# A four-layer transformer with all five engines' orders written in a table: the table is laid out anew

## What is computed

```
x = x + L0_xattn(ctx, ctx, layernorm(x))   # one head, softmax over 120 context rows
x = x + L0_ffn(layernorm(x))               # 8 heads x 8 experts for v and for o, top-2 gates, 128x128 attention
x = x + L1_xattn(layernorm(x), ctx)        # 16 heads, padding masks
x = x + L1_ffn(layernorm(x))               # ternary weights, gelu, 512 hidden
x = x + L2_xattn(layernorm(x), ctx)        # 2 heads, normalised q and k, pair mask
x = x + L2_ffn(layernorm(x))               # 8 experts, top-2, gelu
x = x + L3_xattn(layernorm(x), ctx, bias)  # 16 heads of 64
x = x + L3_ffn(layernorm(x))               # grouped top-2 of 8 experts, relu squared, plus a shared part
```

## Time and profile before

| | us |
|---|---|
| median of 3 executions | 735.09 (734.54 to 735.96) |
| the profiled execution's own time | 735.45 |
| its span, first to last instruction | 734.1 |
| busy: TensorE, VectorE, ScalarE, GpSimd | 666.4, 526.9, 381.2, 197.5 |

### The profile page before, as it was taken

How to read it: one execution, slowest core, us unless ns; L and a number is a source line. 1 busy time by engine, 2 the same in 40 slices (tenths; PEclk the granted TensorE clock), 3 DMA queues, 4 the chain that set the end, 5 groups by cost and what they waited for, 6 DMA issues and landing times.

```text
span 734.1 us, 14783 instructions
## 1 busy us (share of the span) xinstructions
PE 666.4 (91%) x5494; PEld 590.2 (80%) x5494; DVE 526.9 (72%) x1449; ACT 381.2 (52%) x1295; POOL 197.5 (27%) x260
## 2 busy tenths in 40 slices
PE   5859997989999899888999999888999999788987
PEld 4649995759999788667999998577999999467876
DVE  3956657878677928987885677888884777646756
ACT  3431205772354842885457640876538531667583
POOL 1000226411215512532333311622413110542140
PEclk9889999899999989999999999999999999799989
DMA  9859993029963603007755464005766272000000
GB/s 333 332 160 362 397 379 99 2 75 357 319 221 116 230 1 90 3 4 263 272 187 165 147 230 149 1 12 202 243 212 209 101 232 78 5 1 0 2 1 12
DMA packets 34199, 113.86 MB, mean 155 GB/s; under 512 B 4560, under 2 KB 8272, under 8 KB 33744
## 3 DMA queue, kind: packets, MB, share of 16 engines
q1 hardware_dynamic: 34128, 112.92, 43.8%
HBM read 111.86 MB, written 1.05 MB: 154 GB/s over the span
## 4 chain that ended last, share of the span: by engine, by line
PE 65%; DVE 15%; ACT 10%; DMA 4%; POOL 3%; issue 2%; SPq 0%; DVEq 0%; ACTq 0%
PE f_bank L441 31%; PE bank L441 28%; DMA gated<-gates_of 3%; PE bank L679 3%; ACT wide_b L1110 3%; ACT f_b L1018 2%; DVE wide_b L1416 2%; POOL wide_b L1317 2%; DVE max_neg L1675 2%; DVE gated L1413 2%; ACT wide_a L961 1%; DVE f_route L1413 1%; DMA wide_b<-in_raw0f 1%; DVE x L1416 1%; ACT f_a L961 1%
## 5 line engine op out<-in xcount | busy, mean ns | idle before, releaser
L441 PE MATMUL f_bank<-weights,gated 128*128 128x128 f32 x2048 | 246.4, 278 | 7.6 <-DVE gated L1413 7.6
L441 PEld LDWEIGHTS f_bank<-weights,gated 128*128 128x128 f32 x2048 | 236.7, 193 | 11.1 <-issue 8.3
L1110 ACT ACTIVATE wide_b<-wide_b,max_neg 128x120 f32<-128x120 f32 x272 | 103.5, 385 | 22.2 <-DVE max_neg L1768 14.0
L1317 POOL TENSOR_TENSOR wide_b<-wide_b,row_inv 128x480 f32<-128x480 f32 x64 | 69.5, 1091 | 116.2 <-DVE row_inv L1680 116.1
L1413 DVE TENSOR_TENSOR gated<-gated,f_b 128x1024 f32<-128x1024 f32 x64 | 81.2, 1291 | 18.0 <-DMA gated<-gates_of 8.9
L1413 DVE TENSOR_TENSOR gated<-gated,f_xnT 128x1024 f32<-128x1024 f32 x64 | 77.1, 1225 | 19.2 <-DMA gated<-gates_of 18.4
L1309 POOL TENSOR_TENSOR rstd<-var_eps,w_const 128x1 f32<-128x1 f32 (+1 forms) x48 | 35.8, 749 | 194.3 <-DVE var_eps L1409 194.2
L961 ACT ACTIVATE wide_a<-bank 120x512 f32<-120x512 f32 (+4 forms) x110 | 59.3, 544 | 51.9 <-PE bank L679 24.5
L679 PE MATMUL bank<-w_const,wide_b 128*120 128x128 f32 x256 | 44.4, 307 | 14.3 <-POOL wide_b L1317 14.2
L679 PEld LDWEIGHTS bank<-w_const,wide_b 128*120 128x120 f32 x256 | 32.0, 153 | 26.5 <-issue 16.9
L1110 ACT ACTIVATION_READ_ACCUMULATOR wide_b<-wide_b,max_neg 128x1 f32 x272 | 51.8, 190 | 0.0
(11 more groups left out here) (248 smaller groups left out, 1261.7 us busy)
## 6 DMA issues: line engine op xcount, KB each, us to landing
gated<-gates_of SPq DMA_DIRECT2D x128, 512.0 KB, 5.6
weights<-in_experts SPq DMA_DIRECT2D x64, 512.0 KB, 6.3
w_L2f<-in_L2f SPq DMA_DIRECT2D x1, 2124.0 KB, 14.6
w_L3x<-in_L3x SPq DMA_DIRECT2D x1, 2108.0 KB, 18.5
wide_b<-in_raw0f SPq DMA_DIRECT2D x1, 1024.0 KB, 7.3
w_L3f<-in_L3f SPq DMA_DIRECT2D x1, 1000.0 KB, 21.2
w_L1f<-in_L1f SPq DMA_DIRECT2D x1, 516.0 KB, 10.3
x_next<-in_x SPq DMA_DIRECT2D x4, 128.0 KB, 4.9
```

Of the source, the lines that this page charges most:

```text
L441: return nc.tensor.matmul(o, lhsT, rhs, start=first, stop=last)
L1110: last = nc.scalar.activation(p, p, ACT.Exp, bias=max_neg[lane][:, h:h + 1], accum_out=row_sum[lane][:, h:h + 1])
L1317: nc.gpsimd.tensor_tensor(p3, p3, row_inv[lane][:, 4 * i:4 * i + 4].unsqueeze(2).broadcast_to([128, 4, K]), ALU.mult).then_inc(probs_norme ...
```

## The change

Nothing but the table `ORDER` changes. All five strings are written anew; each keeps its length, and each stream keeps its steps and their order within the stream, so every engine executes the same steps as before. What changes is how the three streams are interleaved. The first line of TensorE's string, for example:

```diff
-    "PE": "fff0ffffff0f0f0ffff0ffff0f00fff0ffffffffffff0fffffffffffffffffffffffffffff0f010f1fff0f0ff10f00f1fff0"
+    "PE": "ffffffffff00f0fffffffff0f0ff00fffff00ffffff0fffffffffffffffffffffffffffffff0010f1ff0fff1f0f010f0f0f0"
```

More of the change, by code:

```diff
@@ L63 @@
-    "Pool": "fff0010fff0ff01101001f0f111000111110000110101010110101101010ffff0f0100f0f101111000111100100010000101"
-          "10010111111ff0fff0110000ff101101011010100010010100001110111111ff100f1111100f001111000101010000100011"
+    "PE": "ffffffffff00f0fffffffff0f0ff00fffff00ffffff0fffffffffffffffffffffffffffffff0010f1ff0fff1f0f010f0f0f0"
+          "fff0ff011ff101fff11f1ff1ff01101001010f0ff0ff0f01f01f1ff01f100f1ff1f001f1f0110f1f100010f1f0f11010101f"
+          "110f1fff0f1f110f1f1001010110100f0f001f1ff00110f010fff10ff10fff01f0ff0ff10ff0f1f11f11f00f1f01fff010f1"
+          "f001011011010fff00f01ff0f00110000f0010ff01f10100101ff0f1110f00f0f011f101f1011f0ff10ff1ff0f10f11f1f10"
+          "1f111f1f0f1ff100f0101fff1f1ff00f1f00ffff0f0f0fff1001f1f1ff11f011ff0f0f110010011001ff01010f1f0f0000f0"
+          "0110100f1f10101010ff01f011fff110ff10f0101f0110f010ff0ff1f011ff1f101ff1f101f1f010ff1ff110110110101110"
+          "11011001101011110101000101010001011100011010001000000101010010101100100101010011101011001101011",
@@ new lines @@
+    "Activation": "fffffffffff0fff0fffff0ffffff0f0fff00000ff0ff0fffff00f1ff0f1ff0f0000100f10fff1ff00fff0111fff11ff1ff1f"
+          "1fff1010110001000f1101f01101f1f0f010ff1011f010110010111000110111110000110001001011010f01fff1f0ff00f0"
+          "100f1ff0f01f1f01fff1101f1ff10f0f1f1f0ff1ff0101010101010001f001010f0101010100010000f0ff010f1101ff0100"
+          "11101111011111111001f0f1ff01ff00f01f001fff00f1f0f0fff111fff010f1f1f1f0f1f1ff100110001101010010000101"
+          "10f1f10100100010f010f010f10ff0f110111001101110111110110110111110110100100111001101101110001010000110"
+          "01100100001010010100100001010010111001111101001011101",
@@ new lines @@
+    "DVE": "ffffffffff0f0ffffffffffff0ffff0ffffffffffffff0fffffffffffffffffffffffffffff0ff00f1f0f000ff010ff1f111"
+          "f1fffff10ffff1fffffffffff1ff0100010f0ff1f1f0f0f01fff0f10f10ffff1011011010f101f000100111fff11ff001101"
+          "101f0100f10f1ffffff10100101001001101011fff0f10ff0f10ff0f0001f0ff1f0111f1ffff10f1ffffffffffff1ff10f0f"
+          "f00100111f0ff0ff10f0f0f1f0f00f010000f0101f0111f1f1f00100010011011f0fff0101110f0f111ff1f00ff0fff10f11"
+          "1101111f1ff0fff01f00f1f0f010f00f1ff0f111f1ffff0f0ff1ffff1ffffffff01fff01000111f0f0f1f00f01f101f0f000"
+          "0001100f01ff11ff10f00100111100ff101f101ff1111f1f0010f0f0f00ffff0f11f11101f11f110fff10f11111110101000"
+          "00101111100101000101100100101111100101000000001100000010101111101000000010111111011101",
@@ L65 @@
+    "Pool": "fff100101fff0ff100010f0f110101011100101001100011111011001010ffff0f01001f0f01110110011010010010101010"
+          "10000111111ffff0f10000ff01111001010110101000101100010101101111fff101011110f0001111000101010000100011"
           "1011",
-    "SP": "fffffffffffffffffffffffffffffffffffffffffffffffffffffffff0ffffffffffffffffff1ffffffffffffffffff0ffff"
-          "fff0ffffffff1ffffff1ff01ffffffffffffffffffffffffff1fff0ffff0011ffff",
+    "SP": "fffffffffffffffffffffffffffffffffffffffffffffffffffffffffff1fffffffffffffffff0ff0fffffffffffff1fffff"
+          "fffff1fff0ffffffffff1fffffffffff0fff0fff1ffffffffffffffffff10ff01ff",
```

## The result

| | before | after |
|---|---|---|
| median, us | 735.53 (4 executions) | 723.66 (4 executions) |
| lowest to highest | 734.54 to 737.76 | 722.63 to 726.09 |
| ratio, 95% interval | | 0.9834 (0.9807 to 0.9861) |
| a second series of the new order | 735.89 | 721.57, ratio 0.9809 (0.9770 to 0.9848) |
| profiled execution: time, span | 735.45, 734.1 | 723.76, 722.5 |

What follows compares the result with a forecast made beforehand. TensorE, busy 666.4 of 734.1 us, was taken as the bound, with only its idle 67.6 us to win. Terms −0.4 −0.5 −0.3 −2.0 = −3.2 gave 732.25, 731.9 as a median, stated as 732.0; range 727.0 to 738.0.

Steps and rivals of the forecast that it cites:

- 240 to 290 us: First round's L3X softmax: three more expert steps fill TensorE's 2.79 us wait for GpSimd; −2.0 us, ends −3.3 and +1.0.
- Rival D: At 256.70 us the gap only moves ahead of the first turning; −2.0 becomes −0.5, time 733.5 to 734; chance 0.10.
- 165 to 240 us and its like: Full stretches: six of 27 table loads go, freeing ScalarE of 7.7 us; −0.3 us, ends 0 and −2.7.
- 458 to 510 us: Thin stretch: only neighbours swap, which shifts a wait to the other lane; 0 us, ends −2 and +2.
- 117 to 165 us: Thin stretch: most of TensorE's 2.45 us wait for ScalarE's `exp` goes; −0.5 us, ends −2.45 and +1.2.
- Head: Start: first gates ready sooner, second gates' copy saves VectorE's 0.39 us wait; −0.4 us, ends −1.0 and +0.6.
- 290 to 345 us and the tail: Thin stretch and kernel's end: the new order only swaps neighbours; 0 us each, ends −2 and +2.
- Table loads: On ScalarE, a sign that the forecast is right: 21 table loads and ScalarE busy for about 373.5 us.
- SyncE: Moved loads and stores hold up no spread; first round's later context load keeps some 3 us of cover; 0 us.
- Rival C: Before each round's first expert step: second gates late, 1.2 us in each of three rounds; slower, 738 us; chance 0.20.
- Rival B: A tenth of 41 us TensorE idle in thin windows and tail also goes, 4 us more: 728 us; chance 0.16.

Runs made afterwards that it cites:

- e10: Old order with one TensorE step moved, the first set-up product from raw0f behind six more front steps: 735.84 us, ratio 1.0009 against the old order.
- e1: Old order with the new one in the head alone (to about 110 us): 735.26 us, ratio 0.9981 against the old order.
- e11: Old order with the new one from about 457 to 506 us alone: 735.99 us, ratio 1.0009 against the old order.
- e3: Old order with the new one from about 288 to 457 us alone (round 2): 733.74 us, ratio 0.9969 against the old order.
- e4: Old order with the new one from about 457 us to the end (round 3 and tail): 734.24 us, ratio 0.9981 against the old order.
- e15: Old order up to 288 us, new order behind (rounds 2 and 3, tail): 731.67 us, ratio 0.9939 against the old order.
- e5: Old order with three expert steps put between the first round's L3X softmax turnings, on TensorE alone: 739.87 us, ratio 1.0051 against the old order.
- e7: New order with six table loads put back, 27 again: 723.93 us, ratio 0.9838 against the old order.
- e12: The new order unchanged, measured and profiled again: 721.57 us, ratio 0.9809 against the old order.
- e8: New order with the old one from 110 to 160 and 288 to 338 us: 726.59 us, ratio 0.9872 against the old order.
- e13: New order everywhere except the head (to about 110 us), which has the old one: 722.54 us, ratio 0.9818 against the old order.
- e6: Old order with expert steps between the L3X turnings and the new lane order there, on TensorE and GpSimd: 739.37 us, ratio 1.0043 against the old order.
- e2: Old order with the new one from about 110 to 288 us alone (round 1): 731.15 us, ratio 0.9934 against the old order.
- e9: Old order with the new one from about 160 to 288 us alone: 729.78 us, ratio 0.9926 against the old order.

## Why the prediction was wrong

The direction was right, and most of the idle time that went lay in gaps that I had read. The size failed at these steps.

*240 to 290 us, −2.0 with an end at −3.3.* This was the step that failed most. The end "all idle time of the window" is no bound, as the gap also takes the clock. Measured by the same steps: −5.2 to the end of the softmax and +0.6 behind it. The idle time of the softmax stage fell by 2.3 us, and the rest is the clock and the overlap lost at the gap. How much the clock adds varies with the execution. In e10, which has the old order here, the same gap of 2.79 us stands

```profile
257.72 1.06 PE L679 MATMUL bank<-w_const,wide_b 128*120 128x128 f32 x8 [2.79 <-POOL wide_b L1317]
```

with eight turnings in 1.06 us, and the clock stays full:

```profile
250.00:255.00 5.00, 4.73 (x42) 1.00 0.95 340
255.00:260.00 5.00, 2.28 (x26) 1.00 0.27 108
260.00:265.00 5.00, 5.00 (x58) 1.00 0.01 3
```

The stage is then 17.6 us long (e1, e10, e11); with 1.7 us of full clock lost in it 19.1 (e3, e4, e15), and with 3.4 lost 20.3 (before). With the new order it is 15.1 in all eight profiles that have it. So the gap is worth 2.5 us, and the clock behind it 0 to 2.7 more. The earlier trace rows showed a granted clock of 0.93 for this window, 3.5 us of full clock in 50, and I didn't ask where they lay. Rival D's mechanism, which I gave 0.1, is real for a filler on TensorE alone (e5). It didn't come about here: GpSimd began 3.8 us ahead of the point where the stage starts on TensorE, and 1.7 us behind it before.

*165 to 240 us and its like, −0.3 with an end at −2.7.* Measured −2.7 in round 1 alone, −1.1 in round 2, −0.4 in round 3, 4.2 in all. The term was too small, and so was its end: I took the products' idle time as the room, 2.7 us in three stretches. I had quoted the rule of the Trainium skill (Perfetto Trace Analysis, Identifying the Most-Contended Engine) that the weight loads' busy share tells TensorE's room, and put it aside. The windows of this case agree with the rule: the weight loads' idle time fell by 2.48, 0.83 and 0.47 us in the three stages, and their lengths by 2.7, 1.0 and 0.4, while the products' idle time fell by 1.63, 0.20 and 0.21. My sentence that between expert steps no gap showed was right for expert steps; the room lay at back steps. Whether table loads have a share in it, e7 leaves between 0 and 3.8 us.

*458 to 510 us, 0 with ends of −2 and +2.* Measured −3.1, and −1.5 to −3.9 in the eight profiles with the new order here (47.1 to 49.5 us). The step that failed is "a swap of neighbours shifts a wait to the other lane". Before, TensorE's waits were longest for these:

```profile
PE bank L679 <- POOL wide_b L1317: 2.8, 5, 0.9
PE f_bank L541 <- ACT f_a L961: 1.1, 1, 1.1
```

and after:

```profile
PE bank L679 <- POOL wide_b L1317: 1.0, 3, 0.6
PE f_bank L512 <- ACT f_b L1018: 0.9, 1, 0.9
```

The turnings' waits for GpSimd fell from 2.8 us to 1.0, and nothing like them came up elsewhere: idle time 8.6 to 4.4.

*117 to 165 us, −0.5 with ends of −2.45 and +1.2.* The gap of 2.45 us became two of 0.77 and 0.27 in the profile after, and TensorE's idle time in the stage fell by 2.4 to 2.6 us in both profiles. The stretch's length was 46.7 us in four profiles with the new order and 51.0 and 51.2 in two, against 48.6 to 51.7 with the old one; the means are 48.2 and 50.0, so −0.5 was rather too small. In the first profile after, a long one, the clock is at half from 124 to 139 us, in that of e12 only from 122 to 126. Hence also my wrong expectation that this loss belonged to the order (e8).

*Head, −0.4.* Not told from nothing (e13), so neither confirmed nor refuted. The way was another than I gave: the first spread came at 42.98 us, 2.1 sooner and ahead of my 44 to 45.5, and 0.5 us of that was left at the head's end. *290 to 345 us and the tail, 0:* within 1.2 us in both profiles. *Table loads:* 21, ScalarE busy 373.2 us, as forecast. *SyncE, 0:* no wait for a context load shows in any of the profiles' waits. *Rival C* didn't come about: the spread behind a round's second gates, on the chain before at 159.75 us (6.11) and 333.44 (4.69), is not on it there in either profile of the new order. *Rival B* was nearest, but 728 is 4 us short, and it looked in the wrong place: the thin stretches and the tail gave 2.5 us of the 11.6 by which the first profile is shorter, the full stretches 4.2 and the softmax 5.2.

The range failed because its low end was made of idle time alone. Had each gap that goes been priced with the half clock that follows it, and the full stretches by the weight loads, the low end would have been lower by the clock's 2.7 us at the one gap and by a share of the 15.5 us of room that I had worked out from the weight loads and used in rival B alone.

## What to carry to other kernels

In this kernel a gap on TensorE cost its own length, the overlap of the products around it, and the half clock that may follow; price all three before calling a window's idle time the bound. Where one engine waits for another in a fixed order, moving filler on the waiting engine alone can only move the wait (e5); what helped here was an earlier start of the chain that it waits for, with the other engines' order laid to match. To compare two orders of the same steps, cut both traces where the same set of steps is done: differences of 0.4 us then stand out in single profiles, and stages that vary from run to run are told from those that don't.

## What was not expected of the hardware

The same gap brought the half clock in one execution and not in another. Full clock lost (length times what the granted clock lacks of 1) is 0, 1.7 or 3.4 us in the softmax stage of the old order, behind the same 2.79 us of idle time, and 0, 1.7 or 6.8 us in thin 1 with the new order. The profiles have 19 to 33 us of it in total, 25.8 in the one of e12 that is 18 us shorter in span than before.

These totals leave out the start. The records of the clock begin with its first rise, and the windows show 1.00 ahead of it, yet the products' starts lie 0.21 us apart there and 0.11 behind it; 0.21 is also what they show where the record has the half clock, so the head starts at it. This tells old heads apart. In five profiles (before, e6, e11, e13, e15) the first rise comes at 13.4 to 14.8 us, the first spread at 45.07 to 45.68, and the head ends at 111.1 to 112.6; in five others (e2, e3, e4, e5, e9) the rise comes at 29.1 to 30.1, the spread at 47.00 to 47.69, and the head ends at 114.2 to 115.8. The landing of the first transfers moves the front's first maximum, 12.85 to 13.69 us, but not this: e4 and e15 both have the product from raw0f at 10.24 us and the maximum at 13.41, but the next eight set-up products take 1.92 and 1.06 us, and the first spread comes 2.3 us later in e4. These products in e4:

```profile
15.84 1.92 PE L441 MATMUL bank<-wide_b 128*128 128x128 f32 x8
```

and in e15:

```profile
15.57 1.06 PE L441 MATMUL bank<-wide_b 128*128 128x128 f32 x8
```

With the new head, which doesn't wait for that landing, the first spread comes at 42.96 to 44.47 us and the head ends at 108.4 to 111.3 in six profiles.
